# Expert groups of a mixture-of-experts stage: 57 groups of 256 rows and 21 of 128 in place of 71 of 256, with unrolled loops

## The reference

```python
def _L0_ffn_ref(x, ..., w1, b1, w2, b2):       # T = 8192, D = 128, E = 8, H = 512, K = 2
    logits = _ln(xf, router_ln_scale, router_ln_bias) @ router_w.T + router_b
    probs = jax.nn.softmax(logits, axis=-1)
    topw, topi = jax.lax.top_k(probs, K)
    topw = topw / jnp.sum(topw, axis=-1, keepdims=True)
    gates = jnp.zeros((T, E), xf.dtype).at[jnp.arange(T)[:, None], topi].set(topw)
    def expert(ls, lb, W1, B1, W2, B2):
        h = jax.nn.gelu(_ln(xf, ls, lb) @ W1.T + B1, approximate=False)
        return h @ W2.T + B2
    ys = jax.vmap(expert)(expert_ln_scale, expert_ln_bias, w1, b1, w2, b2)
    out = jnp.einsum('te,etd->td', gates, ys)
...
x = x + jnp.tanh(g_xattn[0]) * L0_xattn(...);  x = x + jnp.tanh(g_ffn[0]) * L0_ffn(...)
x = x + jnp.tanh(g_xattn[1]) * L1_xattn(...);  x = x + jnp.tanh(g_ffn[1]) * L1_ffn(...)
```

## Time and profile before

| what | value |
|---|---|
| median of 3 runs | 1615.91 us (1614.13 to 1621.37) |
| span of the profiled execution, first to last instruction | 1602.7 us |
| of it layer0, up to the last scatter | 445.6 us |
| of it expert_groups, first transpose to last take_y | 454.9 to 733.4 us |
| of it attention_ffn | 742.8 us on |
| TensorE busy | 1480.6 us, 92% |
| VectorE, ScalarE, GpSimd busy | 1177.7, 990.6, 693.3 us |

### The profile page before, as it was taken

The page is one execution under the profiler, slowest core; times in us unless marked ns, Lnnn a source line. Parts: engine busy times, 40 slices in busy tenths (PEclk is TensorE's granted clock), DMA queues, the critical chain, the costliest instruction groups (busy, mean ns, idle before and its releaser), DMA issues.

```text
span 1602.7 us, 51795 instructions
## 1 busy us (share of the span) xinstructions
PE 1480.6 (92%) x20229; PEld 1223.7 (76%) x20229; DVE 1177.7 (73%) x3089; ACT 990.6 (62%) x1990; POOL 693.3 (43%) x605
## 2 busy tenths in 40 slices
PE   4999999999559999996999999999999999999987
PEld 2777777777559999995778777887878777888864
DVE  5688888899623222234688999989999899988875
ACT  3687777876223444442566676666767766677756
POOL 2234666676711111144665545444544544333310
PEclk9799999998679999998999999999999999999999
DMA  9999970000166777761100000000000000000000
GB/s 291 399 388 384 373 248 25 25 32 25 52 222 210 231 229 225 233 187 37 32 24 19 19 19 23 24 23 22 22 22 26 22 22 22 12 12 12 14 9 24
DMA packets 95626, 169.90 MB, mean 106 GB/s; under 512 B 11984, under 2 KB 43728, under 8 KB 95152
## 3 DMA queue, kind: packets, MB, share of 16 engines
q1 hardware_dynamic: 82800, 140.35, 26.4%
q0 software_dynamic: 11600, 26.10, 4.9%
q10 hardware_dynamic: 1008, 0.40, 0.1%
HBM read 75.71 MB, written 91.10 MB: 104 GB/s over the span
## 4 chain that ended last, share of the span: by engine, by line
PE 26%; DVE 19%; issue 6%; ACT 2%; POOL 1%; DMA 1%; DVEq 0%; ACTq 0%
PE L1psY L1263 4%; PE L1psY L1256 4%; PE L1psM L1305 3%; PE L1psY L1248 3%; DVE L1sc L1681 2%; PE L1psS L1274 2%; PE L1psT L1297 2%; DVE L1den L1692 2%; DVE L1am L1743 1%; PE L1psT L1283 1%; DVE x L1573 1%; DVE L1psF L1714 1%; DVE L1hc L1722 1%; POOL yr L1839 1%; PE L1psF L1334 1%
## 5 line engine op out<-in xcount | busy, mean ns | idle before, releaser
L980 ACT ACTIVATE GhT<-GpsH,Gwx 128x256 f32<-128x256 f32 x284 | 118.6, 470 | 158.9 <-PE GpsH L948 157.5
L1436 ACT ACTIVATE L1KT<-L1psY 128x512 f32<-128x512 f32 x128 | 77.5, 606 | 221.9 <-PE L1psY L1248 220.3
L1824 POOL TENSOR_TENSOR L1sc<-L1sc,L1top 128x1024 f32<-128x1024 f32 x64 | 121.8, 1903 | 212.8 <-DVE L1top L1688 212.8
L1829 POOL TENSOR_TENSOR L1sc<-L1sc,L1rden 128x1024 f32<-128x1024 f32 x64 | 121.8, 1904 | 175.5 <-DVE L1rden L1697 175.5
L836 POOL TENSOR_TENSOR L0sc<-L0sc,L0top 128x1024 f32<-128x1024 f32 x64 | 121.6, 1900 | 159.0 <-DVE L0top L566 158.9
L996 DVE TENSOR_TENSOR yg<-GpsY,Gwx 128x256 f32<-128x256 f32 x71 | 30.1, 425 | 168.7 <-PE GpsY L956 168.4
L1248 PE MATMUL L1psY<-cx,L1WK 128*128 128x128 f32 x1024 | 137.5, 278 | 12.0 <-DVE L1identh L1764 12.0
L1256 PE MATMUL L1psY<-L1xnT,L1WQ 128*128 128x128 f32 x1024 | 142.4, 283 | 0.0
L956 PEld LDWEIGHTS GpsY<-Gwx,GhT 128*128 128x128 f32 x1136 | 137.6, 192 | 3.3
L842 POOL DMA_INDIRECT rows_in<-L0xr,slot x128 | 124.7, 974 | 34.0 <-issue 30.5
L1081 POOL DMA_DIRECT2D rows_out<-yg x71 | 38.9, 547 | 230.3 <-issue 230.3
(11 more groups left out here) (310 smaller groups left out, 3668.3 us busy)
## 6 DMA issues: line engine op xcount, KB each, us to landing
Gwx<-in_experts SPq DMA_DIRECT2D x71, 579.0 KB, 4.0
rows_in<-L0zero SPq DMA_DIRECT2D x1, 33792.0 KB, 93.1
rows_out<-L0zero SPq DMA_DIRECT2D x1, 33792.0 KB
Gxg<-rows_in SPq DMA_DIRECT2D x71, 128.0 KB, 3.5
rows_out<-yg POOLq DMA_DIRECT2D x71, 128.0 KB, 3.8
cx<-in_ctxT SPq DMA_DIRECT2D x64, 64.0 KB, 1.8
out<-X SPq DMA_DIRECT2D x64, 64.0 KB, 1.7
L0ctxT<-in_ctxT SPq DMA_DIRECT2D x1, 2560.0 KB, 18.9
```

The source lines that it names most:

```text
L980: nc.scalar.activation(hT[:, u, m, :], psH[:, u, m, :], ACT.Gelu, bias=wx[:, w, ob1 + m:ob1 + m + 1]).then_inc(s["h_ready"], 1)
L1824: nc.gpsimd.tensor_tensor(sc[:, t % SR, :, :], sc[:, t % SR, :, :], broad(top[:, t % 2, :]), ALU.subtract).then_inc(s["shifted"], 1)
L1829: nc.gpsimd.tensor_tensor(sc[:, t % SR, :, :], sc[:, t % SR, :, :], broad(rden[:, t % 2, :]), ALU.mult).then_inc(s["probs_ready"], 1)
```

## The change

Three things. First, the split of the work: 57 groups of 256 rows ("pairs" of 128-row blocks, `NPAIR`) and 21 groups of one block (`NSING`), 78 steps in place of 71. An expert's full pairs come first, capped so that the sum is 57; its rest goes to single blocks. The singles stand at the steps t with t % 8 in (2, 4, 7), up to t = 55; the last 22 steps are all pairs. Second, the table of the singles is built on VectorE with running sums (a scan over the experts, then comparisons with 21 numbers), beside that of the pairs. Third, `pipelined` with its hardware loops gives way to `stepped`, which writes all 78 steps out on every engine. `EARLY_AT` becomes NGR - 12 = 66 and `early_norm` stands at t = 74.

```diff
-NGR = 2 * T // (GE * P) + E - 1
+NPAIR = (2 * T - E * (GE * P - 1) + GE * P - 1) // (GE * P)
+NSING = (2 * T + E * (P - 1)) // P - GE * NPAIR
+NGR = NPAIR + NSING
+SINGLES = [t for t in range(NGR) if t % 8 in (2, 4, 7)][:NSING]
+COLUMN = [NPAIR + SINGLES.index(t) if t in SINGLES else t - sum(i < t for i in SINGLES) for t in range(NGR)]
...
-def pipelined(eng, n, stages, turns=4, first=0, last=0):
+def stepped(n, stages):
     depth = max(lag for lag, _ in stages)
...
-    with eng.Fori(first // turns, (n - last) // turns) as i:
-        for turn in range(turns):
-            step(turns * i + turn, turn, 0, depth)
...
+    for s in range(n + depth):
         for lag, fn in stages:
+            if 0 <= s - lag < n:
+                fn(s - lag, (s - lag) % 2, (s - lag) % XB)
...
-            link(vec.tensor_scalar(groups[:], groups[:], ROUND, None, ALU.subtract))
+            link(vec.tensor_scalar(parts[:], parts[:], ROUND, None, ALU.subtract))
+            link(vec.tensor_tensor_scan(whole[:], ones[:, 0:E], parts[:, 0, :], 0.0, ALU.mult, ALU.add))
+            link(vec.tensor_tensor(room[:], parts[:, 0, :], whole[:], ALU.subtract))
+            link(vec.tensor_scalar(room[:], room[:], float(NPAIR), 0.0, ALU.add, ALU.max))
+            link(vec.tensor_tensor(groups[:], room[:], parts[:, 0, :], ALU.min))
...
+            link(vec.tensor_tensor_scan(start9[:, 1:E + 1], ones[:, 0:E], rest[:], 0.0, ALU.mult, ALU.add))
...
+            link(vec.tensor_tensor(from9[:], group_no[:, 0:NSING].unsqueeze(2).broadcast_to([P, NSING, E + 1]),
+                                   start9[:].unsqueeze(1).broadcast_to([P, NSING, E + 1]), ALU.is_ge))
...
-        EARLY_AT = (NGR - TAIL) // 8 * 8 + 4
+        EARLY_AT = NGR - 12
+        def blocks(t):
+            return 1 if t in SINGLES else GE
...
-                for i in range(GE):
+                for i in range(blocks(t)):
                     last = nc.tensor.transpose(psX[:, i * P:(i + 1) * P], xg[:, w, i, :], ident[:])
...
-                        last = mm(psH[:, u, m, :], wx[:, w, m * P:(m + 1) * P], xT[:, u, :], start=True, stop=True)
+                        last = mm(psH[:, u, m, 0:blocks(t) * P], wx[:, w, m * P:(m + 1) * P], xT[:, u, 0:blocks(t) * P], start=True, stop=True)
...
-            pipelined(pe, NGR, [(0, turn), (1, hidden), (1, weight_sums), (2, project)], turns=8, first=16)
+            stepped(NGR, [(0, turn), (1, hidden), (1, weight_sums), (2, project)])
```

More of the change, by code:

```diff
@@ L52, in wait @@
     eng.wait_ge(sem, value)
-def pipelined(eng, n, stages, turns=4, first=0, last=0):
+def stepped(n, stages):
     depth = max(lag for lag, _ in stages)
-    first = max(first, 4 + depth)
-    first += -first % turns
-    def step(s, turn, lo, hi):
+    for s in range(n + depth):
         for lag, fn in stages:
-            if lo <= lag <= hi:
-                fn(s - lag, (turn - lag) % 2, (turn - lag) % 4, (turn - lag) % 8)
-    for s in range(first):
-        step(s, s, 0, s)
-    with eng.Fori(first // turns, (n - last) // turns) as i:
-        for turn in range(turns):
-            step(turns * i + turn, turn, 0, depth)
-    for s in range((n - last) // turns * turns, n + depth):
-        step(s, s, max(0, s - n + 1), depth)
+            if 0 <= s - lag < n:
+                fn(s - lag, (s - lag) % 2, (s - lag) % XB)
 def build(nc, a, out):
@@ L815, in _ @@
             for h in range(2):
-                vec.tensor_scalar(onehot[:, h, :], group_no[:], place[:, h:h + 1], None, ALU.is_equal).then_inc(s["spread"], 1)
-            link(vec.tensor_reduce(total[:], groups[:], AX.X, ALU.add))
-            link(vec.tensor_scalar(extra[:], group_no[:], total[:, 0:1], float(E * EG), ALU.subtract, ALU.add))
-            link(vec.scalar_tensor_tensor(extra[:], extra[:], float(E * EG), extra[:], ALU.is_ge, ALU.mult))
+                vec.tensor_scalar(onehot[:, h, :], group_no[:, 0:NPAIR], place[:, h:h + 1], None, ALU.is_equal).then_inc(s["spread"], 1)
@@ new lines, in _ @@
+            link(vec.scalar_tensor_tensor(rest[:], groups[:], -float(GE), parts[:, 1, :], ALU.mult, ALU.add))
+            vec.memset(start9[:, 0:1], 0.0)
+            link(vec.tensor_tensor_scan(start9[:, 1:E + 1], ones[:, 0:E], rest[:], 0.0, ALU.mult, ALU.add))
+            link(vec.tensor_scalar(shift9[:, 0:E], groups[:], float(GE), None, ALU.mult))
+            link(vec.scalar_tensor_tensor(shift9[:, 0:E], base[:], 1.0 / P, shift9[:, 0:E], ALU.mult, ALU.add))
+            vec.memset(shift9[:, E:E + 1], float(E * XROWS // P - MINSING))
@@ L822, in _ @@
-            steps3[0] += 1
-            link(vec.tensor_tensor(row_group[:], psR[:, 0:NGR], extra[:], ALU.add))
+            vec.tensor_scalar(owner[:, 0:NPAIR], psR[:, 128:128 + NPAIR], 0.0, None, ALU.add)
+            link(vec.tensor_scalar(row_group[:, 0:NPAIR], psR[:, 0:NPAIR], 0.0, None, ALU.add))
             vec.tensor_tensor(m2[:], m2[:], m1[:], ALU.subtract).then_inc(s["apart"], 1)
@@ L979, in gelu, with take_x @@
                         wait(act, s["h_ps"], 2 * t + m // 2 + 1)
[L980 removed]
+                    nc.scalar.activation(hT[:, u, m, 0:blocks(t) * P], psH[:, u, m, 0:blocks(t) * P], ACT.Gelu,
                                          bias=wx[:, w, ob1 + m:ob1 + m + 1]).then_inc(s["h_ready"], 1)
[L982 removed]
+            stepped(NGR, [(0, gelu)])
         @block.vector
         def _(dve):
[L986 removed]
+            def take_x(t, u, w):
                 wait(dve, s["x_ps"], t + 1)
@@ L1072, in early_norm, with store, fetch @@
                     link(vec.scalar_tensor_tensor(y, b, 1.5, y, ALU.add, ALU.mult))
-            pipelined(dve, NGR, [(0, take_x), (3, collect), (2, take_y), (3, early_norm), (1, prepare)], turns=8, first=16, last=TAIL)
+            stepped(NGR, [(0, take_x), (3, collect), (2, take_y), (3, early_norm), (1, prepare)])
         @block.gpsimd
         def _(pool):
-            def store(t, u, z4, w):
+            def store(t, u, w):
                 wait(pool, s["y_ready"], t + 1)
                 pool.sem_inc(passed, 1)
-                g = pool.value_load(row_group[0:1, bass.ds(t, 1)], min_val=0, max_val=XGROUPS - 1)
+                c, n = COLUMN[t], blocks(t)
+                g = pool.value_load(row_group[0:1, c:c + 1], min_val=0, max_val=(XGROUPS if n == GE else XBLOCKS) - 1)
+                rows_out = pairs_out if n == GE else blocks_out
                 pool.dma_start(rows_out[bass.ds(g, 1), :, :].rearrange("g p f -> p g f"),
-                               yg[:, u:u + 1, :, :].rearrange("p o i d -> p o (i d)")).then_inc(y_out[u], 16)
-            def fetch(t, u, z4, w):
+                               yg[:, u:u + 1, 0:n, :].rearrange("p o i d -> p o (i d)")).then_inc(y_out[u], 16)
+            def fetch(t, u, w):
                 i = early_tile(t)
@@ L1095, in fetch @@
                                                  ).then_inc(early_in[i], 16)
-            pipelined(pool, NGR, [(0, fetch), (0, store)], turns=8, last=TAIL)
+            stepped(NGR, [(0, fetch), (0, store)])
 def attention_ffn(nc, a, X, ident, gate, att, ffn, weight, slot, ys, early, out):
```

76 lines of the change are left out of this document (44 added, 32 removed).

## The result

The changed kernel took **1600.15 us** (median of 20 runs, 1589.09 to 1613.44), the kernel before 1608.38 us beside it (20 runs, 1599.04 to 1621.48). The ratio is 0.9937, 95% interval 0.9908 to 0.9965: faster by 0.6%. In a later comparison, 1594.12 us (12 runs) stood against 1601.37 (17 runs), ratio 0.9959, interval 0.9930 to 0.9988: faster by 0.4%. The forecast was 1602.1 us with a range of 1597.5 to 1609.5, as a gain of 13.8 us; the two medians differ by 8.2 and 7.3 us.

The account below looks back on a forecast made before the run. TensorE's own instructions were taken to bound the expert stage. Pairs and singles -12.1 us and the stage's end -1.7 us gave -13.8 us, from 1615.91 to 1602.1 us, other terms 0; range for 8 in 10: 1597.5 to 1609.5.

Parts of the forecast that it names:

- What bounds the stage: Expert stage: TensorE's own instructions set its length, 3.732 us a step, until another chain takes over.
- Pairs and singles: Expert stage: 14 pairs go at 3.732 us each, 21 singles come at 1.91 us each, together -12.1 us.
- cost 0, with the round trip below as a rival: Mixed steps: DMA volume at 264 GB/s does not bind, cost 0; the stores' round trip was kept as a rival.
- landings of the stores near 4.1: Sign expected in the trace after: result stores landing in about 4.1 us, against 3.8 at the median before.
- The link (1.77 + L): Two result buffers: take_y 0.42 us, 1.35 to the store's issue, then landing L; four links must fit eight steps.
- mild A: Rival A, the stores' round trip becomes the bound; mild form: landings 4.4 to 4.7 us, time 1605 to 1613, chance 0.10.
- C: Rival: small semaphore waits of 0.1 to 0.3 us in each single step, 4 us in all, time 1606; chance 0.08.
- The volume: Mixed steps: eight move 6296 KB in 24.4 us, 264 GB/s, DMA share about 0.85; does not bind, cost 0.
- The table: End of layer0: under 5 us more on VectorE, hidden by 10.6 us of cover under GpSimd's last scatter; cost 0.
- Loops written out: Expert stage: writing out all steps neither gains by fewer branches nor loses by code fetch; 0 us.
- The end of the stage: Last steps: early_norm's chain one step earlier is covered by TensorE's work, so the last store moves up; -1.7 us.
- rival B: Hidden part of singles: half a group costs more than half; +8.7 us, time 1610.8; chance 0.04.

Follow-up runs that it names:

- c2_after: The changed kernel with nothing altered, profiled again in a later execution; all 45 store landings in the window listed, 4.3 us at the median (3.4 to 5.3).

## Why the prediction came out as it did

**What bounds the stage.** Right. TensorE kept 148.57 of 150 us in the mixed steps, and the parts of a step came as worked out: 0.89 for a single's hidden part against 0.90, 24.49 us for eight steps against 24.4.

**Pairs and singles, -12.1 us.** The work is sized right; with three buffers, where the landings hold nothing, the stage is 263.4 and 264.5 us, 1.3 and 0.2 under the forecast of 264.7. With two the term lost 3.3 us to the store's round trip, 1 to 5 by the execution.

**The step that failed** is "cost 0, with the round trip below as a rival", and within it "landings of the stores near 4.1". The link (1.77 + L) and its limit (4.3) were right; L was 4.3, and the spread mattered more than the median. Half of the landings are over the limit when the median stands on it (22 of 45 in the profile that has all), and the prediction priced only a median over it, seven cycles of 4 x (L - 4.3). The mean was on the limit too, 4.32, and nothing built up: that profile's TensorE lost 0.3 us of 140 in the mixed steps. What TensorE sees is single late landings. So neither the forecast nor mild A came true in full: it is the mechanism of A, at 3.3 us, less than half of the 8.4 that its mild form costs at L = 4.6. Small waits by themselves (C) it was not, since a third buffer removed them. The hope that single stores land sooner for being half as large didn't come true: 4.31 us against 4.33.

**The volume.** 260 GB/s and 0.85 against 264 and about 0.85: right, and it did not bind. But the landings rose with it. In one execution (`c2_after`) they took 4.3 us at the median at 262 GB/s and 3.9 in the pairs behind, at 239; 3.8 was the value at 228 GB/s before. That the load is what lengthened them is likely and not shown, since no run varied it alone.

**The table.** 9.4 us of cover, cost 0: right. The last scatter did not stay where it was, but moved with the execution and not with the table: VectorE made its last rows for the scatters at 420.2 and the last scatter began 17.2 us later, 17.0 before.

**Loops written out.** 0, right, by the run that did that alone: 186.60 us for 50 steps against 186.62.

**The end of the stage, -1.7 us.** Right: the last `take_y` came 1.8 us behind TensorE's end before and comes at once now, in the changed kernel and in the run that moved it alone. The waits for the fetched rows came back at the same size, as said (1.17 us in place of 1.24).

**What the prediction didn't have.** It took the barrier's 7.7 us as a constant behind the last store, which is right within 0.6 us (7.7 to 8.3), and didn't ask whether the drain has to start there. The runs on the drain found 6.9 us there for nothing but another queue.

**Half a group costs half (rival B).** 0.89 against 1.73 us. The Trainium skill's spacing (TensorE: Matmul & The Clock Gate, "Back-to-back issue gap"), 81 ns at 128 columns and 131 at 512, would give 1.44 us as an estimate. Float32 matmuls of 128 columns followed each other every 0.112 us here, those of 256 every 0.216. The trace decides for the ratio of one half.

**The time.** 13.8 us forecast, -10.45 + 0.6 = -9.9 in the profile, 8.2 between the medians. The time of 1600.15 lies 2 us under the forecast only because the comparison's kernel before was itself 7.5 us faster than the median on which the forecast was built; that the time came out so near is luck. The 13.2 us "around the span" were of the same kind: in every execution that lists both, the time is 1.6 to 2.4 us more than the span, so the profiled execution of the kernel before was simply faster than the median of its three runs.

## What to carry to other kernels

When work per step is cut, list every chain that goes once around a ring of buffers and divide its round trip by the number of buffers: if that comes within a tenth of a step, price the spread of the transfer, not its median, and count a third buffer as part of the change. Spread short steps among long ones. And look behind a stage's last instruction: an engine that is last to finish there should not be the one whose barrier work is longest.

## What the runs showed of the hardware

- GpSimd's drain behind this block took 7.7 to 8.3 us, with stores under way (7747, 8320 ns) or with none (7742). At other barriers it took 2.35 and 11.16 us; what sets it is open. SyncE's behind its own stores took 13 ns, with the landings awaited ahead of it.
- The landing of a store issued by GpSimd took 3.8 us at the median at 228 GB/s and 4.3 at 260 to 262 GB/s (3.4 to 5.3), for 64 KB as for 128 KB.
- TensorE's granted clock has no record ahead of 39 to 40 us in seven profiles and ahead of 55 to 56 us in the seven others, and the view prints 1.00 there. By the matmuls it was at the lower of its two levels: 655 ns each, as at a recorded 0.50, against 398 at a recorded 1.00.
